# A graph kernel's second aggregation: six PSUM banks for the sums, two shared by the pairs' products, and weighted one-hots in batches of eight

## The chip, the cores and the metric

The kernel runs on one core of a Trainium2 chip. The metric is the device time of one execution in microseconds (us).

## The reference

Four blocks act in turn on x (6250 nodes, 256 columns, float32): a graph layer, a feed-forward layer with eight experts, a second, weighted graph layer with a small MLP behind it, and a second expert layer. 100,000 edges connect the nodes. The change lies in the third block:

```python
def _L1_gnn_ref(h6_all, edge_index, edge_weight, W, b, W1, b1, W2, b2):
    N = h6_all.shape[0]
    row, col = (edge_index[0], edge_index[1])
    sl = jnp.arange(N, dtype=edge_index.dtype)
    row_sl = jnp.concatenate([row, sl])
    col_sl = jnp.concatenate([col, sl])
    ew_sl = jnp.concatenate([edge_weight, jnp.ones((N,), dtype=edge_weight.dtype)])
    deg = jax.ops.segment_sum(ew_sl, row_sl, num_segments=N)
    dinv = jnp.where(deg > 0, jax.lax.rsqrt(deg), 0.0)
    norm = dinv[row_sl] * ew_sl * dinv[col_sl]
    xw = h6_all @ W
    msgs = xw[col_sl] * norm[:, None]
    h7 = jax.ops.segment_sum(msgs, row_sl, num_segments=N) + b
    h = jax.nn.relu(h7 @ W1 + b1)
    out = h @ W2 + b2
    return out
...
x = x + _L0_gnn_ref(_layernorm(x, axis=-1), src, dst, L0_gnn_W_src, L0_gnn_gamma, L0_gnn_beta)
x = x + _L0_ffn_ref(_layernorm(x, axis=-1)[None], L0_ffn_W1, L0_ffn_b1, L0_ffn_Wg, L0_ffn_bg, L0_ffn_Wd, L0_ffn_bd)[0]
x = x + _L1_gnn_ref(_layernorm(x, axis=-1), edge_index, edge_weight, L1_gnn_W, L1_gnn_b, L1_gnn_W1, L1_gnn_b1, L1_gnn_W2, L1_gnn_b2)
x = x + _L1_ffn_ref(_layernorm(x, axis=-1)[None], L1_ffn_Wg, L1_ffn_bg, L1_ffn_bias, L1_ffn_W1, L1_ffn_b1, L1_ffn_W2, L1_ffn_b2)[0]
```

## The kernel before, in words

Nodes are held in 49 tiles of 128. The edges, sorted by the node that receives the sum, are cut into 830 items (ITEMS) of at most 128 edges of one tile. An aggregation treats one item at a time:

- POOL gathers 128 rows of 256 floats from DRAM with an indirect DMA into one of 12 ring buffers (`aggregate_gpsimd`, L772). Gather i waits until the sum of item i-12 is made.
- DVE makes a one-hot matrix, 128 edges x 128 nodes of the tile.
- PE multiplies it with the gathered rows into a PSUM bank (`aggregate_tensor`, L761; in the trace each float32 matmul is two records).
- DVE adds the bank into the tile's accumulator (`add_sums`, L728), whose offset it reads into registers once in eight items.

Each engine runs a program of its own, in order, and waits on semaphores. `sum_made` counts PE's sums, `added` DVE's adds. The first layer's aggregation (some 150 to 1467 us) takes four banks by turns and makes unweighted one-hots for eight items with one instruction (`one_hots`, L713), in two halves of `hot1`. Beside it run other works of the set-up for the second layer, among them the comparison L783 and the product L785 on DVE. The second layer's aggregation (some 2996 to 4209 us) takes two banks and makes the one-hot of item i+2, times the edge weight, with one instruction per item (`one_hot`, L720), in four buffers.

What follows the sums in the second layer is done in pairs of tiles beside it, in `heads` of `second_vector`, `second_scalar` and `second_tensor`. A pair has steps 0 to 10, and a table of due items says beside which item each is issued. On this input it is `when_on_time` (L1591): step n of pair gi is due at item 17 x (tiles up to and with the pair) + 11 + 3n, so that a pair's steps are three items apart and pairs 34 items. The steps are: 0 scale by the degree (DVE, L1648); 1 transpose (PE, L1755, bank 2); 2 copy out (DVE, L1641); 3 product and bias (PE L1704, ACT L1696, bank 3); 4 the same with Relu (PE L1704, ACT L1687, bank 4); 5 third product (PE, L1735, bank 5); 6 add to x and statistics (DVE, L1632, L543); 7 normalize (DVE, L568); 8 transpose (PE, L1160, bank 6; ACT L1677); 9 gate product (PE, L1716, bank 7); 10 gate's bias and the search for the two best experts (DVE, L1608 to L1616). The loop goes on behind item 829 until the last pair is done; the last pair (gi = 24) is a single tile.

```python
m.wait_ge(ring_in[i % RING], 16 * (ring_loads(l, i % RING) + i // RING + 1))
if i >= nbank:
    m.wait_ge(added, l * ITEMS + i - nbank + 1)
m.matmul(bank[i % nbank][:, 0:width], lhsT=hot,
         rhs=ring[:, i % RING, 0:width], start=True, stop=True).then_inc(sum_made, 1)
beside(i)
```

## Time and profile before

| | us |
|---|---|
| median of 3 runs | 4848.15 (4842.85 to 4851.48) |
| the profiled execution | 4810.92 |
| its span | 4809.2 |
| busy in the span: PE, DVE, ACT, POOL | 3136.0, 2361.0, 1010.2, 2867.8 |
| mean granted clock of TensorE | 0.76 |

The span runs from the first to the last instruction of the profiled execution. Busy times are unions of an engine's instructions; those that only wait, branch or issue a DMA from another queue are not in them. In a group of instructions the idle time is that of the engine just before each of them, followed by what ended it; "issue" is idle time for which the profile shows no releaser, "remote" one that it can't name. The granted clock is a share of full speed: 1.0 is 2.4 GHz, 0.5 is 1.2 GHz.

### The profile page before, as it was taken

The numbers are of one execution on the slowest core, as the hardware profiler recorded it, in microseconds if no ns is written. First come the engines' busy times: TensorE is split into PE (matmuls) and PEld (weight loads), VectorE is DVE, ScalarE is ACT, GpSimd is POOL, SyncE is SP. The second block draws the span as 40 slices with busy tenths as digits, with TensorE's granted clock in tenths as the row PEclk, the third lists the DMA queues.
The fourth block names the chain that finished last, engine by engine and source line by source line (L and its number), as shares of the span: only waits on it lengthen the run. The fifth ranks groups of instructions, "written<-read, shape, count | busy, mean of one in ns | idle before, by whom it ended". The sixth has DMA issues, their size and how long they took to land.

```text
span 4809.2 us, 46065 instructions
## 1 busy us (share of the span) xinstructions
PE 3136.0 (65%) x11900; PEld 2202.3 (46%) x11900; DVE 2361.0 (49%) x5924; ACT 1010.2 (21%) x2504; POOL 2867.8 (60%) x2727
## 2 busy tenths in 40 slices
PE   4666778776772111067786872666666666669997
PEld 3555656655541111034466662344444444456555
DVE  6578777787861000144434115455555555553332
ACT  3444544444410000022230012000000000012221
POOL 1566777788877777700003661666666666647776
PEclk8777776678765555578897886678777877789999
DMA  3332333322231000011122334333333333433332
GB/s 122 91 89 74 90 90 90 90 84 80 80 84 38 1 1 1 1 70 57 70 79 72 108 103 148 97 98 103 100 104 100 100 104 100 99 118 56 53 56 45
DMA packets 201342, 378.28 MB, mean 79 GB/s; under 512 B 58955, under 2 KB 125783, under 8 KB 200696
## 3 DMA queue, kind: packets, MB, share of 16 engines
q0 software_dynamic: 134080, 283.48, 22.3%
q1 hardware_dynamic: 57964, 82.57, 4.9%
q10 hardware_dynamic: 9036, 9.15, 0.6%
q8 instruction: 114, 1.87, 0.2%
q14 instruction: 148, 1.21, 0.1%
HBM read 301.05 MB, written 75.83 MB: 78 GB/s over the span
## 4 chain that ended last, share of the span: by engine, by line
PE 40%; issue 17%; DVE 16%; another core or an unknown queue 13%; POOL 8%; DMA 3%; ACT 2%; DVEq 1%; SPq 0%; POOLq 0%; ACTq 0%
PE bank L761 18%; PE bank L1324 5%; DVE acc_or_weights L728 4%; PE bank L1513 4%; POOL out_rows L1930 3%; PE bank L1160 3%; PE bank L948 2%; POOL ring_or_weights L772 2%; PE bank L1704 2%; PE bank L1341 2%; POOL normed L1907 2%; POOL normed L1911 1%; PE bank L965 1%; DMA ring_or_weights<-gather_table,item_other_node 1%
## 5 line engine op out<-in xcount | busy, mean ns | idle before, releaser
L772 POOL DMA_INDIRECT ring_or_weights<-gather_table,item_other_node x1660 | 1753.4, 1056 | 830.7 <-issue 458.8
L728 DVE TENSOR_TENSOR acc_or_weights<-bank,acc_or_weights 128x257 f32 (+1 forms) x1660 | 704.3, 424 | 857.7 <-PE bank L761 450.8
L761 PE MATMUL bank<-ring_or_weights,normed 128*128 128x257 f32 x1660 | 769.2, 556 | 243.4 <-issue 162.5
L761 PE MATMUL bank<-ring_or_weights 128*128 128x256 f32 x1660 | 656.1, 513 | 386.3 <-DVE acc_or_weights L728 200.2
L1136 POOL DMA_INDIRECT items_by_src<-edge_records_by_src,edge_positions x542 | 553.7, 1022 | 169.1 <-issue 165.5
L761 PEld LDWEIGHTS bank<-ring_or_weights 128*128 128x128 f32 x1660 | 339.9, 241 | 658.8 <-issue 633.7
L948 PEld LDWEIGHTS bank<-normed,acc_or_weights 128*128 128x128 f32 x1564 | 393.2, 259 | 220.8 <-ACT acc_or_weights L941 90.4
L761 PEld LDWEIGHTS bank<-ring_or_weights,normed 128*128 128x128 f32 x1660 | 351.4, 260 | 309.0 <-issue 287.5
L1160 PE MATMUL bank<-identity,normed 128*128 128x128 f32 x1764 | 276.3, 288 | 281.9 <-DVE normed L568 221.6
L939 ACT ACTIVATE acc_or_weights<-iota_row,ring_or_weights 128x128 f32<-128x128 f32 x782 | 315.2, 403 | 647.5 <-PE bank L948 488.4
L948 PE MATMUL bank<-normed,acc_or_weights 128*128 128x49 f32 x1564 | 330.1, 301 | 89.1 <-ACT acc_or_weights L941 56.5
L1464 POOL DMA_INDIRECT normed<-hidden_rows,item_weight x56 | 54.7, 977 | 556.1 <-DVE item_weight L1413 537.8
L1160 PEld LDWEIGHTS bank<-identity,normed 128*128 128x128 f32 x1764 | 211.0, 146 | 375.8 <-DVE normed L568 144.3
L1174 PE MATMUL bank<-normed,ones 128*128 128x256 f32 x96 | 56.5, 690 | 401.2 <-issue 401.2
L720 DVE TENSOR_SCALAR ring_or_weights<-iota_row,item_local_node,item_weight 128x128 f32<-128x128 f32 x830 | 289.4, 349 | 3.2 <-issue 3.2
L1513 PE MATMUL bank<-acc_or_weights,normed 128*128 x896 | 226.0, 408 | 48.2 <-issue 30.6
L941 ACT ACTIVATE acc_or_weights<-acc_or_weights 128x128 f32<-128x128 f32 x782 | 243.6, 311 | 24.9
L1200 DVE SCALAR_TENSOR_TENSOR acc_or_weights<-acc_or_weights,normed 128x256 f32<-128x256 f32 x49 | 23.7, 484 | 430.6 <-issue 419.6
L1324 PE MATMUL bank<-ring_or_weights,normed 128*128 128x512 f32 x392 | 233.8, 753 | 0.0
L1174 PEld LDWEIGHTS bank<-normed,ones 128*128 128x128 f32 x96 | 23.8, 304 | 432.9 <-issue 432.5
L1513 PEld LDWEIGHTS bank<-acc_or_weights,normed 128*128 128x128 f32 x896 | 179.4, 206 | 79.9 <-issue 54.4
L1930 POOL DMA_INDIRECT out_rows<-normed,item_weight x105 | 169.3, 1612 | 76.3 <-issue 52.5
(348 smaller groups left out, 4106.1 us busy)
## 6 DMA issues: line engine op xcount, KB each, us to landing
ring_or_weights<-gather_table,item_other_node POOLq DMA_INDIRECT x1660
hidden_rows<-normed SPq DMA_DIRECT2D x49, 512.0 KB
items_by_src<-edge_records_by_src,edge_positions POOLq DMA_INDIRECT x542
acc_or_weights<-in_L_ffn_Wd SPq DMA_DIRECT2D x8, 1024.0 KB
acc_or_weights<-in_L_ffn_W SPq DMA_DIRECT2D x16, 512.0 KB, 9.8
gather_table<-normed SPq DMA_DIRECT2D x7, 896.0 KB, 4.1
gather_table<-acc_or_weights SPq DMA_DIRECT2D x7, 896.0 KB, 4.0
gather_table<-normed SPq DMA_DIRECT2D x24, 256.0 KB
```

What stands on the lines that cost most here:

```text
L720: v.tensor_scalar(onehot[:, i % 4, :], iota[:, :], dloc[:, i:i + 1], wt[:, i:i + 1], ALU.is_equal, ALU.mult).then_inc(hot_made, 1)
L728: v.tensor_tensor(into, bank[i % nbank][:, 0:width], into, ALU.add).then_inc(added, 1)
L761: m.matmul(bank[i % nbank][:, 0:width], lhsT=hot, rhs=ring[:, i % RING, 0:width], start=True, stop=True).then_inc(sum_made, 1)
L772: g.indirect_dma_start(ring[:, i % RING, 0:D], None, table, IndirectOffsetOnAxis(ap=gidx[:, i:i + 1], axis=0)).then_inc(ring_in[i % RING], 16)
L939: s.activation(lo_tmp, iota[:, :], ACT.Abs, bias=neg_lo[:, i:i + 1]).then_inc(lo_abs, 1)
L941: s.activation(lo_hot[:, i % 2, :], lo_tmp, ACT.Relu, bias=1.0, scale=-1.0).then_inc(lo_done, 1)
L948: m.matmul(bank[7][:, 0:T], lhsT=lo_hot[:, j % 2, :], rhs=tile_hot[:, j // HOTS % 2, j % HOTS, :], start=j == 0, stop=j == EC - 1).then_in ...
L1136: g.indirect_dma_start(item_d, IndirectOffsetOnAxis(ap=idx1[:, c:c + 1], axis=0), rec1[:, c, :], None).then_inc(edge_scattered[k], 16)
L1160: last = m.transpose(to[:, k * P:(k + 1) * P], rows[:, k * P:(k + 1) * P], ident[:, :])
L1324: last = m.matmul(bank[2 + half][:, :], lhsT=xt[:, u % 2, k * P:(k + 1) * P], rhs=w1a[:, k, cols], start=k == 0, stop=k == KD - 1)
L1513: last = m.matmul(bank[4 + u % 2][:, 0:D], lhsT=ht[:, u % 2, c * P:(c + 1) * P], rhs=wd[:, ds(regs[u // 4][u % 4] + c * D, D)], start=c == ...
L1930: g.indirect_dma_start(out, IndirectOffsetOnAxis(ap=to_row[:, u:u + 1], axis=0), ys1[:, u % 4, :], None, bounds_check=N - 1, oob_is_err=Fa ...
```

## The change

In the second layer six banks serve the sums. The steps of the pairs share banks 6 (PING: steps 1, 4 and 8) and 7 (PONG: steps 3, 5 and 9), and their waits are those for the last reader of the same bank. One-hots are made for eight items at once: a comparison as in the first layer, then a product in place with the edge weights, in two halves of a new buffer `hot2`. The last pair's due items are counted as if it had two tiles, 17 items later than before. The table for late input changes too; it isn't used here.

```diff
...
     ring = view(R, 0, RING * AW).rearrange("p (n a) -> p n a", a=AW)
-    after_ring = 4 * RING * AW
-    onehot = view(R, after_ring, 4 * P).rearrange("p (n c) -> p n c", c=P)
     def space(off, n, dt=F32, parts=P):
...
     xt2 = space(12288, 2 * G2 * D).rearrange("p (n a) -> p n a", n=2)
+    hot2 = space(24576, 2 * HOTS * P).rearrange("p (n c) -> p n c", c=P)
     norm2 = space(16384, 3 * G2 * D).rearrange("p (n t d) -> p n t d", n=3, d=D)
...
 
-    def one_hots(b):
+    HOT_BATCHES = -(-ITEMS // HOTS)
+    def one_hots(l, b):
         n = min(HOTS, ITEMS - b * HOTS)
+        cols = slice(b * HOTS, b * HOTS + n)
         if b >= 2:
-            v.wait_ge(sum_made, (b - 1) * HOTS)
-        at = b % 2 * HOTS
-        v.tensor_tensor(hot1[:, at:at + n, :], iota[:, :].unsqueeze(1).broadcast_to([P, n, P]),
-                        dloc[:, b * HOTS:b * HOTS + n].unsqueeze(2).broadcast_to([P, n, P]),
-                        ALU.is_equal).then_inc(hots_in, 1)
-
-    def one_hot(i):
-        if i >= 4:
-            v.wait_ge(sum_made, ITEMS + i - 3)
-        v.tensor_scalar(onehot[:, i % 4, :], iota[:, :], dloc[:, i:i + 1], wt[:, i:i + 1],
-                        ALU.is_equal, ALU.mult).then_inc(hot_made, 1)
+            v.wait_ge(sum_made, l * ITEMS + (b - 1) * HOTS)
+        hot = (hot1, hot2)[l][:, b % 2 * HOTS:b % 2 * HOTS + n, :]
+        equal = v.tensor_tensor(hot, iota[:, :].unsqueeze(1).broadcast_to([P, n, P]),
+                                dloc[:, cols].unsqueeze(2).broadcast_to([P, n, P]), ALU.is_equal)
+        if l == 0:
+            equal.then_inc(hots_in, 1)
+        else:
+            equal.then_inc(hots_in, 1)
+            v.wait_ge(hots_in, HOT_BATCHES + 2 * b + 1)
+            v.tensor_tensor(hot, hot, wt[:, cols].unsqueeze(2).broadcast_to([P, n, P]), ALU.mult).then_inc(hots_in, 1)
 
...
     def aggregate_vector(l, width, nbank, beside):
-        if l:
-            one_hot(0)
-            one_hot(1)
-        else:
-            one_hots(0)
+        one_hots(l, 0)
         regs = {}
         for i in range(ITEMS):
-            if l and i + 2 < ITEMS:
-                one_hot(i + 2)
-            if not l and i % HOTS == 1 and (i // HOTS + 1) * HOTS < ITEMS:
-                one_hots(i // HOTS + 1)
+            if i % HOTS == 1 and (i // HOTS + 1) * HOTS < ITEMS:
+                one_hots(l, i // HOTS + 1)
             beside(i)
...
         for i in range(ITEMS):
-            if l:
-                m.wait_ge(hot_made, i + 1)
-                hot = onehot[:, i % 4, :]
-            else:
-                m.wait_ge(hots_in, i // HOTS + 1)
-                hot = hot1[:, i % (2 * HOTS), :]
+            m.wait_ge(hots_in, HOT_BATCHES + 2 * (i // HOTS) + 2 if l else i // HOTS + 1)
+            hot = (hot1, hot2)[l][:, i % (2 * HOTS), :]
             m.wait_ge(ring_in[i % RING], 16 * (ring_loads(l, i % RING) + i // RING + 1))
...
     def when_late(gi, n):
-        return ITEMS + gi + n
+        return ITEMS + 12 * gi + n
 
     def when_on_time(gi, n):
-        return PER_TILE * min(T, G2 * (gi + 1)) + MARGIN + 1 + STEP * n
+        return PER_TILE * G2 * (gi + 1) + MARGIN + 1 + STEP * n
 
...
 
+    SUM_BANKS, PING, PONG = 6, bank[6], bank[7]
     def second_vector(when):
...
                 v.wait_ge(g_mm, gi + 1)
-                v.tensor_tensor(logits1[:, a:a + n, :], bank[7][:, 0:n * 8].rearrange("p (t e) -> p t e", e=8),
+                v.tensor_tensor(logits1[:, a:a + n, :], PONG[:, 0:n * 8].rearrange("p (t e) -> p t e", e=8),
                                 bg1.unsqueeze(1).broadcast_to([P, n, 8]), ALU.add).then_inc(g_out, 1)
...
                 v.wait_ge(x_mm, gi + 1)
-                v.tensor_tensor(X[:, a:a + n, :], bank[5][:, 0:n * D].rearrange("p (t d) -> p t d", d=D),
+                v.tensor_tensor(X[:, a:a + n, :], PONG[:, 0:n * D].rearrange("p (t d) -> p t d", d=D),
                                 X[:, a:a + n, :], ALU.add).then_inc(x_out, 1)
...
                 v.tensor_copy(at_b[gi % 2][:, :, 0:n * P],
-                              bank[2][:, :].rearrange("p (k n) -> p k n", k=KD)[:, :, 0:n * P]).then_inc(a_in, 1)
+                              PING[:, :].rearrange("p (k n) -> p k n", k=KD)[:, :, 0:n * P]).then_inc(a_in, 1)
             for gi in due(when, 0, i):
...
 
-        aggregate_vector(1, D, 2, beside)
+        aggregate_vector(1, D, SUM_BANKS, beside)
         for i in range(ITEMS, head_ends(when)):
...
                     s.wait_ge(g_mm, gi - 1)
-                s.activation(xt2[:, gi % 2, 0:n * D], bank[6][:, 0:n * D], ACT.Copy).then_inc(g_in, 1)
+                s.activation(xt2[:, gi % 2, 0:n * D], PING[:, 0:n * D], ACT.Copy).then_inc(g_in, 1)
             for gi in due(when, 6, i):
...
                 for c in range(KD):
-                    last = s.activation(ct_b[gi % 2][:, c, 0:n * P], bank[4][:, c * G2 * P:c * G2 * P + n * P],
+                    last = s.activation(ct_b[gi % 2][:, c, 0:n * P], PING[:, c * G2 * P:c * G2 * P + n * P],
                                         ACT.Relu, bias=bcol[:, 2 + c:3 + c])
...
                 for c in range(KD):
-                    last = s.activation(bt_b[gi % 2][:, c, 0:n * P], bank[3][:, c * G2 * P:c * G2 * P + n * P],
+                    last = s.activation(bt_b[gi % 2][:, c, 0:n * P], PONG[:, c * G2 * P:c * G2 * P + n * P],
                                         ACT.Identity, bias=bcol[:, c:c + 1])
...
                 m.wait_ge(g_in, gi + 1)
-                if gi >= 1:
-                    m.wait_ge(g_out, gi)
+                m.wait_ge(x_out, gi + 1)
                 for j in range(n):
                     for k in range(KD):
-                        last = m.matmul(bank[7][:, j * 8:(j + 1) * 8],
+                        last = m.matmul(PONG[:, j * 8:(j + 1) * 8],
                                         lhsT=xt2[:, gi % 2, j * D + k * P:j * D + (k + 1) * P],
...
                 m.wait_ge(applied2, gi + 1)
-                if gi >= 1:
-                    m.wait_ge(g_in, gi)
                 for j in range(n):
-                    last = transpose_rows(norm2[:, gi % 3, j, :], bank[6][:, j * D:(j + 1) * D])
+                    last = transpose_rows(norm2[:, gi % 3, j, :], PING[:, j * D:(j + 1) * D])
                 last.then_inc(g_tr, 1)
...
                 m.wait_ge(c_in, gi + 1)
-                if gi >= 1:
-                    m.wait_ge(x_out, gi)
                 for j in range(n):
                     for k in range(KD):
-                        last = m.matmul(bank[5][:, j * D:(j + 1) * D], lhsT=ct_b[gi % 2][:, k, j * P:(j + 1) * P],
+                        last = m.matmul(PONG[:, j * D:(j + 1) * D], lhsT=ct_b[gi % 2][:, k, j * P:(j + 1) * P],
                                         rhs=gcn_w[2][:, k, :], start=k == 0, stop=k == KD - 1)
...
                 m.wait_ge(b_in, gi + 1)
-                if gi >= 1:
-                    m.wait_ge(c_in, gi)
-                product(bank[4], gcn_w[1], bt_b[gi % 2], pairs[gi][1]).then_inc(c_mm, 1)
+                product(PING, gcn_w[1], bt_b[gi % 2], pairs[gi][1]).then_inc(c_mm, 1)
             for gi in due(when, 3, i):
...
                 if gi >= 1:
-                    m.wait_ge(b_in, gi)
-                product(bank[3], gcn_w[0], at_b[gi % 2], pairs[gi][1]).then_inc(b_mm, 1)
+                    m.wait_ge(g_out, gi)
+                product(PONG, gcn_w[0], at_b[gi % 2], pairs[gi][1]).then_inc(b_mm, 1)
             for gi in due(when, 1, i):
...
                 if gi >= 1:
-                    m.wait_ge(a_in, gi)
+                    m.wait_ge(g_in, gi)
                 for k in range(KD):
                     for j in range(n):
-                        last = m.transpose(bank[2][:, (k * G2 + j) * P:(k * G2 + j + 1) * P],
+                        last = m.transpose(PING[:, (k * G2 + j) * P:(k * G2 + j + 1) * P],
                                            acc[:, a + j, k * P:(k + 1) * P], ident[:, :])
...
 
-        aggregate_tensor(1, D, 2, heads)
+        aggregate_tensor(1, D, SUM_BANKS, heads)
         for i in range(ITEMS, head_ends(when)):
```

Where the order of instructions moves, the rows of both programs say it. In the following blocks each row is one instruction with the tiles it writes and reads; ISA at the add's line and TENSOR_LOAD are register work. First DVE in the second layer beside three items, before:

```order
L720 TENSOR_SCALAR ring_or_weights<-iota_row,item_local_node,item_weight 128x128 [waits rows_summed]
L728 ISA [waits added,rows_summed]
L728 TENSOR_TENSOR acc_or_weights<-bank,acc_or_weights 128x256
L720 TENSOR_SCALAR ring_or_weights<-iota_row,item_local_node,item_weight 128x128 [waits rows_summed]
L1657 TENSOR_TENSOR x_rows<-x_rows,edge_records_by_src 128x256
L96 TENSOR_LOAD item_acc_offset [waits bias_added]
L728 ISA [waits added,rows_summed]
L728 TENSOR_TENSOR acc_or_weights<-bank,acc_or_weights 128x256
```

And DVE of the changed kernel at the start of a group of eight items (its add is L730):

```order
L96 TENSOR_LOAD item_acc_offset
L730 ISA [waits added,rows_summed]
L730 TENSOR_TENSOR acc_or_weights<-bank,acc_or_weights 128x256
L716 TENSOR_TENSOR normed<-iota_row,item_local_node 128x1024 [waits rows_summed]
L723 TENSOR_TENSOR normed<-normed,item_weight 128x1024 [waits hots_set]
L730 ISA [waits added,rows_summed]
L730 TENSOR_TENSOR acc_or_weights<-bank,acc_or_weights 128x256
L730 ISA [waits added,rows_summed]
L730 TENSOR_TENSOR acc_or_weights<-bank,acc_or_weights 128x256
```

The one-hot in front of every add is gone; once in eight items two instructions of 1024 elements a partition stand between two adds. Then PE behind the last item, before (L1755 transposes of step 1, L1704 steps 3 and 4, L1735 step 5, L1160 step 8, L1716 step 9):

```order
L1735 MATMUL bank<-edge_records_by_src,normed 128x256 [waits head_x_out,head_c_in]
L1735 MATMUL bank<-edge_records_by_src,normed 128x256 x3
L1755 MATMUL bank<-identity,acc_or_weights 128x128 [waits head_sums_in,head_scaled]
L1755 MATMUL bank<-identity,acc_or_weights 128x128
L1160 MATMUL bank<-identity,normed 128x128 [waits head_n_in,head_normed]
L1160 MATMUL bank<-identity,normed 128x128 x3
L1704 MATMUL bank<-normed,edge_records_by_src 128x128 [waits head_b_in,head_sums_in]
L1704 MATMUL bank<-normed,edge_records_by_src 128x128 x3
L1716 MATMUL bank<-edge_records_by_src,normed 128x8 [waits head_gate_out,head_n_in]
L1716 MATMUL bank<-edge_records_by_src,normed 128x8 x3
```

The same place of the changed kernel (L1724 step 5, L1152 step 8, L1709 step 9, L1742 step 1, L1698 step 3):

```order
L1724 MATMUL bank<-edge_records_by_src,normed 128x256 [waits head_c_in]
L1724 MATMUL bank<-edge_records_by_src,normed 128x256 x3
L1152 MATMUL bank<-identity,normed 128x128 [waits head_normed]
L1152 MATMUL bank<-identity,normed 128x128 x3
L1709 MATMUL bank<-edge_records_by_src,normed 128x8 [waits head_x_out,head_n_in]
L1709 MATMUL bank<-edge_records_by_src,normed 128x8 x3
L1742 MATMUL bank<-identity,acc_or_weights 128x128 [waits head_n_in,head_scaled]
L1742 MATMUL bank<-identity,acc_or_weights 128x128
L1698 MATMUL bank<-normed,edge_records_by_src 128x128 [waits head_gate_out,head_sums_in]
L1698 MATMUL bank<-normed,edge_records_by_src 128x128 x3
```

The last tile's steps stood between those of the pair before; now they stand behind them.

## Rows read from the trace of the kernel before

**Rows 1.** The page: the span, and from its costliest groups the gathers and the adds.
```profile
span 4809.2 us, 46065 instructions
...
## 5 line engine op out<-in xcount | busy, mean ns | idle before, releaser
L772 POOL DMA_INDIRECT ring_or_weights<-gather_table,item_other_node x1660 | 1753.4, 1056 | 830.7 <-issue 458.8
```

**Rows 2.** Busy time by stretch (us): three of the first layer's aggregation, one of the second's.
```profile
core 0: us, PE busy (x) PEld busy (x) DVE busy (x) ACT busy (x) POOL busy (x), PEclk, DMA share, GB/s
160.00:400.00 240.00, 162.63 (x617) 122.38 (x616) 167.30 (x410) 108.03 (x303) 158.90 (x161) 0.74 0.30 89
600.00:850.00 250.00, 197.94 (x680) 157.66 (x680) 184.31 (x319) 120.75 (x338) 198.47 (x170) 0.68 0.31 90
1100.00:1440.00 340.00, 244.36 (x907) 174.80 (x908) 260.74 (x453) 114.84 (x322) 274.50 (x216) 0.75 0.30 81
3010.00:4200.00 1190.00, 815.79 (x2538) 515.77 (x2537) 660.28 (x2105) 56.94 (x138) 775.53 (x819) 0.77 0.35 100
```

**Rows 3.** Groups of instructions by form, 3010:4200 us.
```profile
line engine op names shapes xcount | busy us, mean ns | idle before us <-releasers
L772 POOL DMA_INDIRECT ring_or_weights<-gather_table,item_other_node x819 | 776.4, 948 | 414.6 <-issue 172.2 <-PE bank L761 172.2 <-remote 70.1
L761 PE MATMUL bank<-ring_or_weights 128*128 128x256 f32 x1626 | 642.9, 513 | 374.2 <-DVE acc_or_weights L728 198.5 <-issue 170.7
...
L720 DVE TENSOR_SCALAR ring_or_weights<-iota_row,item_local_node,item_weight 128x128 f32<-128x128 f32 x813 | 283.7, 349 | 0.0
```

**Rows 4.** The waits, 3010:4200 us.
```profile
engine line waited for: us in total, times, longest us
...
DVE acc_or_weights L728 <- PE bank L761: 304.2, 276, 3.4
PE bank L761 <- DVE acc_or_weights L728: 198.5, 151, 5.1
...
DVE acc_or_weights L728 <- remote: 148.4, 55, 5.5
```

**Rows 5.** Timeline, second layer: start us, duration us, instruction [idle before <-releaser].
```profile
3021.54 1.19 PE L761 MATMUL bank<-ring_or_weights 128*128 128x256 f32 x2 [3.00 <-issue]
...
3025.87 0.42 DVE L728 TENSOR_TENSOR acc_or_weights<-bank,acc_or_weights 128x256 f32 x1 [4.22 <-remote]
...
3026.44 1.19 PE L761 MATMUL bank<-ring_or_weights 128*128 128x256 f32 x2 [3.71 <-DVE acc_or_weights L728]
...
3030.77 0.42 DVE L728 TENSOR_TENSOR acc_or_weights<-bank,acc_or_weights 128x256 f32 x1 [4.22 <-remote]
3030.91 0.94 POOL L772 DMA_INDIRECT ring_or_weights<-gather_table,item_other_node  x1 [3.44 <-remote]
```

**Rows 6.** Groups, POOL, first layer: 160:400, 600:850 and 1100:1440 us, in this order.
```profile
L772 POOL DMA_INDIRECT ring_or_weights<-gather_table,item_other_node x161 | 160.7, 998 | 81.4 <-issue 32.7 <-PE bank L761 28.1 <-remote 20.6
...
L772 POOL DMA_INDIRECT ring_or_weights<-gather_table,item_other_node x170 | 199.1, 1171 | 51.8 <-issue 44.5 <-PE bank L761 7.0 <-remote 0.3
...
L772 POOL DMA_INDIRECT ring_or_weights<-gather_table,item_other_node x202 | 251.6, 1245 | 61.5 <-issue 50.0 <-PE bank L761 11.6
```

**Rows 7.** Timeline, first layer: gathers issued while DVE ran L783 or L713.
```profile
651.12 0.56 DVE L783 TENSOR_TENSOR normed<-iota_row,edge_positions 128x392 f32<-128x392 f32 x1
...
651.31 1.18 POOL L772 DMA_INDIRECT ring_or_weights<-gather_table,item_other_node  x1 [0.30 <-PE bank L761]
...
651.71 0.57 DVE L785 TENSOR_TENSOR normed<-normed,edge_records_by_src 128x392 f32<-128x392 f32 x1
...
671.57 1.22 DVE L713 TENSOR_TENSOR normed<-iota_row,item_local_node 128x1024 f32<-128x1024 f32 x1
671.63 1.98 POOL L772 DMA_INDIRECT ring_or_weights<-gather_table,item_other_node  x1 [0.30 <-issue]
```

**Rows 8.** Line L713: duration ns min/median/max, first and last start us, forms.
```profile
L713 DVE TENSOR_TENSOR normed<-iota_row,item_local_node x104: 948/1216/1225, 150.3 to 1430.1; 128x1024 f32<-128x1024 f32 x103, 128x768 f32<-128x768 f32 x1
```

**Rows 9.** Timeline, the tail of the second layer.
```profile
4209.02 0.42 DVE L728 TENSOR_TENSOR acc_or_weights<-bank,acc_or_weights 128x256 f32 x1 [0.73 <-PE bank L761]
...
4221.13 0.41 DVE L1641 COPY normed<-bank 128x256 f32<-128x256 f32 x1
...
4224.93 0.17 DVE L1608 TENSOR_TENSOR normed<-bank,edge_records_by_src 128x16 f32<-128x16 f32 x1 [3.39 <-PE bank L1716]
...
4234.56 0.16 DVE L1616 FIND_INDEX8 normed<-normed 128x8 uint32<-128x8 f32 x1
```

2 lines of the change are left out of this document (1 added, 1 removed).

## The prediction

> **What bounds the kernel now.** I began with the page: the span is 4809.2 us and the gathers of L772 head its costliest groups [rows 1]. The change touches only the second aggregation, so next came the table by stage. In the stretch 3010:4200, which holds nearly all of that stage, POOL is busy 775.5 of 1190 us, PE 815.8 and DVE 660.3, so no engine is full [rows 2]. The groups of that stretch say what one item costs: 819 gathers of 948 ns, each with its idle time in front, 414.6 us in all [rows 3]. Hence 1190/819 = 1.453 us an item.
>
> How much of that idle time is a wait? In the stretch 600:850 of the first layer 170 gathers have 51.8 us before them, 0.305 each, and in 1100:1440 it is 61.5/202 = 0.304 [rows 6]: that is what POOL itself takes between two gathers. So POOL's own pace is 0.948 + 0.305 = 1.253 us, and the rest, 414.6 - 819 x 0.305 = 165 us (167 for all 830 items), is POOL standing still because the ring of 12 is full. It is full because PE and DVE hold each other: PE waits 198.5 us for L728's adds [rows 4], which free one of two banks, and DVE waits 304.2 us for PE and 148.4 us for something the profile calls remote [rows 4]. The timeline shows the latter: a sum starts at 3021.54 and takes 1.19 us by its record, yet the add that follows comes at 3025.87 after 4.22 us of idle time, the next sum at 3026.44 after 3.71 us, and at 3030.77 and 3030.91 DVE and POOL are released together [rows 5]. PE reports late there, and with two banks nothing else can start meanwhile.
>
> **The change, part by part.**
>
> 1. Six banks instead of two. The sum of item i now waits for the add of item i-6. What can leave is the 167 us. Bounds come from the first layer, which has four banks and the same ring: in 600:850 and 1100:1440 nothing is left over 0.305 us a gather; in 160:400 it is 81.4 - 161 x 0.305 = 32.3 us, 0.20 a gather, which over 830 would be 167 us, all of it [rows 6]. PE's busy share is 0.68 in the stretch that stalls, 0.79 and 0.72 in the two that don't [rows 2]. The second layer has 0.69 now, and with the same work in some 1160 us 0.70 to 0.71, beside the 0.72. I take a fifth as staying, 33 us, for two of three stretches show none: -134 us. The bounds are -167 and 0.
>
> 2. One-hots in batches. Removed are 830 L720 of 349 ns, 290 us of DVE. Added are 104 times two instructions over 1024 elements. The first has the form of L713, 1216 ns [rows 8]; no row shows the second (a product with the weights) at that size, but over 392 elements it takes 0.57 us against 0.56 for the comparison [rows 7], so 1216 again: 104 x 2.43 = 253 us. DVE gets 37 us less, which lies beside PE and POOL and counts nothing.
>
> 3. What the batches do to POOL is the real price. A gather issued 0.06 us after L713 began took 1.98 us, not 0.95, and ended 0.82 us after L713's end [rows 7]. A gather issued s after the start is thus longer by 1.09 - s. Caught at any moment of a cadence of 1.25 us, that is 1.09 x 1.09 / (2 x 1.25) = 0.475 us a batch on average; caught at the start, 1.09. I take the middle, 0.78, since both happen and DVE's place in the cadence follows PE and DVE, not chance. For the second instruction the pair L783, L785 counts: a gather issued inside the first ended 0.82 us after the first's end, though the second was running [rows 7]. So it slips in between, and the next, 0.30 us later, is held by the second for about 0.03. Together 0.81 x 104 = +84 us, bounds 0.475 x 104 = 49 and 1.12 x 104 = 116. L720 was free of this: gathers beside it last 948 ns [rows 3].
>
> The Trainium skill, SBUF — State Buffer, section "Who interferes with whom", says that a DVE instruction with two SBUF inputs and a GpSimd instruction that reads SBUF exclude each other for the whole instruction. It speaks against this change, and the trace agrees with 1.98 us. Read as one lock over both instructions, it would hold a gather for 2.3 - s, on average 1.68 us a batch, an estimate of +175 us instead of +84; the gather of 651.31 decides against that reading.
>
> 4. The block on DVE. For 2.4 us no add runs, and the adds are what frees banks. At 1.35 us an item that is two items, and six banks (or the three items between two steps of a pair) cover it; with two they would not. Nothing is queued there for ACT that is due within three items. A batch is made seven items before PE needs it. At the stage's start batch 0 takes 2.4 us instead of 0.35, beside the first gather and its landing: nothing.
>
> 5. Sharing banks 6 and 7. PE's steps of a pair now wait for a reader of the same bank one or two steps earlier, at least three items before, or for the pair before, four or more items back. In the order nothing is queued closer, so zero while DVE is less than three items behind. It also means that PE leads DVE by three or four items near the steps, not six.
>
> 6. The last pair comes 17 places later, after the pair before is finished. The rows of the tail: the last add at 4209.02, pair 23's logits at 4224.93, the end at 4234.56 + 0.16 [rows 9]. Pair 23's gate product would come up to 1 us earlier without L1704 between, so its search ends by about 4224.7. Then the last tile runs alone: scale 0.34, transposes 0.4, and from its copy at 4221.13 to 4234.72, 13.6 us, less about 1 for the gate product that lay between. That is 4224.7 + 13.9 = 4238.6: +4 us (2 to 6).
>
> **Sum**: -134 + 84 + 4 = -46 us. The profiled execution took 4810.9 us and would take 4765. The median shown is 4848.2, 37 us above it; I carry the difference over: 4802 us.
>
> **Rivals.** (a) Slower: the lateness is PE's own and goes on with six banks, while the lock comes on top. For it speaks 160:400, four banks and 0.20 us of stall a gather [rows 6]; against it the later stretches. Place: PE's reports and the full ring. It decides from 47% of the 167 us staying (167 - 84 - 4 = 79). At three quarters: +46, 4894 us. Chance 0.19.
>
> (b) Slower: PE's granted clock sinks. It is 0.77 here and 0.68 to 0.75 in the first layer [rows 2], the mean of the levels 1.2 and 2.4 GHz. If it stayed at 0.5, an item would take the 1.19 us of [rows 5] and the pairs' work (815.8 - 642.9) x 0.77/0.5 = 266 us: 830 x 1.19 + 266 = 1254 us, above 830 x 1.453 = 1206: +52, 4900 us. It decides where PE's own time passes POOL's 1.35 us an item. The Trainium skill, TensorE: Matmul & The Clock Gate, section "A second HAM failure mode: psum-queue depth-cycling", tells of a kernel whose turns through PSUM banks with short PE idles between kept the clock going up and down. The trace has that up and down with two banks already. Chance 0.05.
>
> (c) The stalls and the lock about cancel (40 to 52% stay): within 10 us of now. Chance 0.10.
>
> (d) All stalls go and the lock costs its lower bound: -167 + 49 + 4 = -114, 4734 us. Chance 0.12.
>
> The forecast has the remaining 0.54.
>
> **Numbers.** A measurement here can tell about 0.2%, 10 us, from no change. Faster: 0.54 + 0.12 = 0.66; same 0.10; slower 0.24. The forecast's own ends: the lock at 116 with a third of the stalls staying (-111 + 116 + 4 = +9) and the lock at 49 with a fifth (-81). The range reaches on into (d) and into (a) up to about two thirds staying: 4745 to 4885.
>
> **What the profile after would show.** L772 in the second layer: mean near 1.05 us (right if 1.01 to 1.09) and idle near 0.35 us each; a mean of 0.95 would refute step 3, idle above 0.45 step 1. Gathers issued just behind a batch comparison last 1.9 to 2.0 us. PE's wait for the adds falls from 198.5 us to under 40. The stage falls from 1.453 to about 1.39 us an item, and the tail from the last add to the last search grows from 25.7 to about 30 us. Wrong altogether: if DVE still stands idle 4 us at a time for PE's reports and POOL stands with it.

## The result and the profile after

The change makes the kernel slower by a quarter of a per cent: 4860.8 us against 4848.7 (medians of 17 runs each), a ratio of 1.0026 with a 95% interval of 1.0016 to 1.0035. Forecast were 46 us less; it is 12 us more. The profiled execution took 4868.6 us, 58 more than that of before, but half of this is not the change: the second aggregation begins at 3025.1 us instead of 2996.3, and all of that stems from instructions that the change leaves alone (the first aggregation takes 1317 us in the profile of before and 1350 in that of the change, and 1310 to 1350 in all profiles of such chips below). The profile of before, 4810.9 us, is also not one of the 17 runs, whose fastest took 4835.6. So the stage itself is what to compare.

**Stage** means here from the start of the first gather of the second aggregation to the end of its last add, **stall** POOL's idle time before its gathers, from the second on, less 0.305 us each, and **tail** from that last add to the end of the last search. Before: stage 1213.1 us, stall 165, tail 25.3. After: stage 1230.0, stall 137, tail 32.1.

The page of the changed kernel, span and gathers of both layers, beside [rows 1]:

```profile
span 4866.8 us, 45372 instructions
...
L764 POOL DMA_INDIRECT ring_or_weights<-gather_table,item_other_node x1660 | 1790.9, 1079 | 814.9 <-issue 472.8
...
L716 DVE TENSOR_TENSOR normed<-iota_row,item_local_node 128x1024 f32<-128x1024 f32 x208 | 252.6, 1214 | 4.3 <-issue 3.6
```

Busy time in the stretch 3039:4229, the same part of the stage as 3010:4200 in [rows 2], with the same columns (the clock is the third number from the end, 0.75):

```profile
3039.00:4229.00 1190.00, 769.83 (x2507) 551.56 (x2506) 680.41 (x1473) 56.23 (x136) 807.96 (x810) 0.75 0.35 99
```

The groups of that stretch, which answer to [rows 3]:

```profile
L764 POOL DMA_INDIRECT ring_or_weights<-gather_table,item_other_node x810 | 808.4, 998 | 382.3 <-issue 185.8 <-remote 103.5 <-PE bank L753 93.0
L753 PE MATMUL bank<-ring_or_weights,normed 128*128 128x256 f32 x1603 | 553.8, 489 | 210.5 <-DVE acc_or_weights L730 128.5 <-issue 64.9 <-DVE normed L723 15.7
...
L730 DVE TENSOR_TENSOR acc_or_weights<-bank,acc_or_weights 128x256 f32 x801 | 339.1, 423 | 502.4 <-remote 212.4 <-PE bank L753 156.4 <-issue 66.2
```

The gathers' mean went from 948 to 998 ns. POOL's idle time per gather went from 0.506 only to 382.3/810 = 0.472 us; 0.35 had been expected. The gather line thus costs 1.470 us an item instead of 1.453. The idle time that was gained is smaller than what the gathers lost. The waits of the stretch, beside [rows 4]:

```profile
DVE acc_or_weights L730 <- remote: 212.4, 67, 8.1
...
DVE acc_or_weights L730 <- PE bank L753: 156.4, 127, 4.5
PE bank L753 <- DVE acc_or_weights L730: 128.5, 78, 4.8
...
PE bank L1724 <- ACT normed L1681: 52.3, 7, 11.8
PE bank L1698 <- ACT normed L1690: 48.5, 8, 8.7
```

PE's wait for the adds fell from 198.5 us, but to 128.5 and not under 40. New are PE's waits at the pairs' steps: with those for DVE (25.0, 16.1 and 10.5) and the 10.0 for ACT at L1709 they are 162 us, where before had none, and 15.7 us for the batches (L723). And DVE still stands for PE, now up to 8.1 us in one piece. The timeline shows such a piece (start us, duration us, instruction, idle before):

```profile
3816.66 1.99 PE L1698 MATMUL bank<-normed,edge_records_by_src 128*128 128x256 f32 x8 [1.12 <-issue]
3817.30 0.42 DVE L730 TENSOR_TENSOR acc_or_weights<-bank,acc_or_weights 128x256 f32 x1 [1.87 <-remote]
...
3818.49 1.46 PE L753 MATMUL bank<-ring_or_weights,normed 128*128 128x256 f32 x6
...
3819.45 0.42 DVE L730 TENSOR_TENSOR acc_or_weights<-bank,acc_or_weights 128x256 f32 x1 [0.27 <-PE bank L753]
...
3827.16 0.84 ACT L1681 ACTIVATE normed<-bank,bias_columns 128x256 f32<-128x256 f32 x2 [10.55 <-remote]
3827.30 0.42 DVE L730 TENSOR_TENSOR acc_or_weights<-bank,acc_or_weights 128x256 f32 x1 [7.42 <-remote]
3827.43 0.95 POOL L764 DMA_INDIRECT ring_or_weights<-gather_table,item_other_node  x1 [2.74 <-remote]
3828.05 3.06 PEld L1724 LDWEIGHTS bank<-edge_records_by_src,normed 128*128 128x128 f32 x8 [8.49 <-ACT normed L1681]
...
3828.47 1.22 DVE L716 TENSOR_TENSOR normed<-iota_row,item_local_node 128x1024 f32<-128x1024 f32 x1
3828.69 1.82 POOL L764 DMA_INDIRECT ring_or_weights<-gather_table,item_other_node  x1 [0.31 <-issue]
3829.72 1.23 DVE L723 TENSOR_TENSOR normed<-normed,item_weight 128x1024 f32<-128x1024 f32 x1
3830.82 0.95 POOL L764 DMA_INDIRECT ring_or_weights<-gather_table,item_other_node  x1 [0.30 <-issue]
```

By its records PE had a pair's product (step 4) done at 3818.65 and three sums at 3819.95. ACT, DVE and POOL hear of them only at 3827.2 to 3827.4, all at once. In the trace the updates of `sum_made` for the three sums stand at 3827.18, 3827.22 and 3827.26, 0.04 us apart, though a sum is four PE instructions; in the second aggregation of before_again, on the second kind of chip below, no two of its updates are nearer than 0.43 us. So here sums seem to have been made before and told late. Free banks don't help: the sums that filled them are reported late too, and PE itself stands at step 5 for ACT, which stood for the product. The last four rows are the lock of step 3: a gather issued 0.22 us after L716's start ends 0.82 us after L716's end, while L723 is running. The one behind it is issued 1.10 us after L723's start, so late that the same rule (1.09 - s) costs it nothing: 0.95 us.

The tail:

```profile
4254.68 0.42 DVE L730 TENSOR_TENSOR acc_or_weights<-bank,acc_or_weights 128x256 f32 x1 [0.96 <-PE bank L753]
...
4287.04 0.16 DVE L1610 FIND_INDEX8 normed<-normed 128x8 uint32<-128x8 f32 x1
```

### The profile page after: what moved, and what is told of

The parts are those of the page before. It is cut to its first block, busy times and chain, and to the rows that moved or that the text cites. A ratio compares the mean times of both kernels' runs of the same rounds, so it can differ in the third digit from the quotient of the medians.

```text
span 4866.8 us, 45372 instructions
## 1 busy us (share of the span) xinstructions
PE 3090.0 (63%) x11900; PEld 2229.2 (46%) x11900; DVE 2391.3 (49%) x5302; ACT 1010.2 (21%) x2504; POOL 2895.4 (59%) x2727
## 4 chain that ended last, share of the span: by engine, by line
PE 31%; issue 25%; DVE 17%; another core or an unknown queue 14%; POOL 7%; ACT 2%; DMA 2%; DVEq 1%; SPq 0%; POOLq 0%; ACTq 0%
PE bank L753 10%; PE bank L1316 5%; PE bank L1505 4%; DVE acc_or_weights L730 4%; POOL out_rows L1917 3%; PE bank L1152 3%; PE bank L940 3%; PE bank L1698 2%; PE bank L1333 2%; POOL normed L1894 2%; POOL ring_or_weights L764 1%; POOL normed L1898 1%; PE bank L957 1%; DVE normed L716 1%
## 5 line engine op out<-in xcount | busy, mean ns | idle before, releaser
L764 POOL DMA_INDIRECT ring_or_weights<-gather_table,item_other_node x1660 | 1790.9, 1079 | 814.9 <-issue 472.8
L753 PE MATMUL bank<-ring_or_weights,normed 128*128 128x257 f32 (+1 forms) x3320 | 1339.7, 521 | 446.5 <-issue 201.0
L730 DVE TENSOR_TENSOR acc_or_weights<-bank,acc_or_weights 128x257 f32 (+1 forms) x1660 | 703.5, 424 | 873.9 <-PE bank L753 309.7
L753 PEld LDWEIGHTS bank<-ring_or_weights,normed 128*128 128x128 f32 x3320 | 731.7, 253 | 665.8 <-issue 527.2
L1128 POOL DMA_INDIRECT items_by_src<-edge_records_by_src,edge_positions x542 | 539.1, 995 | 183.5 <-issue 182.0
L940 PEld LDWEIGHTS bank<-normed,acc_or_weights 128*128 128x128 f32 x1564 | 383.3, 256 | 266.5 <-ACT acc_or_weights L933 147.6
L1152 PE MATMUL bank<-identity,normed 128*128 128x128 f32 x1764 | 278.4, 289 | 310.7 <-DVE normed L568 225.5
L1152 PEld LDWEIGHTS bank<-identity,normed 128*128 128x128 f32 x1764 | 208.5, 146 | 413.4 <-issue 162.9
L1505 PE MATMUL bank<-acc_or_weights,normed 128*128 x896 | 228.5, 411 | 44.8 <-issue 29.0
L716 DVE TENSOR_TENSOR normed<-iota_row,item_local_node 128x1024 f32<-128x1024 f32 x208 | 252.6, 1214 | 4.3 <-issue 3.6
L1879 PE MATMUL bank<-acc_or_weights,normed 128*128 x840 | 198.6, 379 | 1.7 <-ACT normed L1845 1.7
L1871 PE MATMUL bank<-acc_or_weights,normed 128*128 x420 | 199.3, 597 | 0.0
```

What stands on the lines that cost most here:

```text
L716: equal = v.tensor_tensor(hot, iota[:, :].unsqueeze(1).broadcast_to([P, n, P]), dloc[:, cols].unsqueeze(2).broadcast_to([P, n, P]), ALU.is ...
L730: v.tensor_tensor(into, bank[i % nbank][:, 0:width], into, ALU.add).then_inc(added, 1)
L753: m.matmul(bank[i % nbank][:, 0:width], lhsT=hot, rhs=ring[:, i % RING, 0:width], start=True, stop=True).then_inc(sum_made, 1)
L764: g.indirect_dma_start(ring[:, i % RING, 0:D], None, table, IndirectOffsetOnAxis(ap=gidx[:, i:i + 1], axis=0)).then_inc(ring_in[i % RING], 16)
L940: m.matmul(bank[7][:, 0:T], lhsT=lo_hot[:, j % 2, :], rhs=tile_hot[:, j // HOTS % 2, j % HOTS, :], start=j == 0, stop=j == EC - 1).then_in ...
L1128: g.indirect_dma_start(item_d, IndirectOffsetOnAxis(ap=idx1[:, c:c + 1], axis=0), rec1[:, c, :], None).then_inc(edge_scattered[k], 16)
```

## The experiments

The runs fell on several chips, and these are of two kinds. On the first kind the kernel before takes 4819 to 4849 us (medians; the result above is of this kind), on the second 4045 to 4051. The program and its data are the same. Each chip below served one group of runs only, so it is not shown whether the chip makes the difference or the state that it was in then. Every row names the kind, and its ratio is to runs of before on the same chip.

| run | kind | ratio to before (95% interval) | stage us | gather ns | stall us | tail us |
|---|---|---|---|---|---|---|
| before | 1 | | 1213.1 | 948 | 165 | 25.3 |
| the change | 1 | 1.0026 (1.0016 to 1.0035) | 1230.0 | 998 | 137 | 32.1 |
| banks2 | 1 | 1.0076 (1.0063 to 1.0089) | 1248.8 | 997 | 156 | 30.7 |
| banks3 | 1 | 1.0036 (1.0024 to 1.0048) | 1226.0 | 1006 | 128 | 30.2 |
| single6 | 1 | 1.0036 (1.0023 to 1.0048) | 1220.7 | 949 | 168 | 32.0 |
| half_sums_b | 1 | single run | 1210.7 | 1005 | 113 | |
| filler_b | 1 | single run | 1229.3 | 990 | 144 | 30.7 |
| after_again | 1 | 1.0037 (1.0020 to 1.0053) | 1218.7 | 992 | 130 | 34.1 |
| single6_b | 1 | 1.0031 (1.0007 to 1.0055) | 1218.3 | 950 | 163 | 32.0 |
| single2 | 1 | 1.0016 (1.0004 to 1.0028) | 1225.6 | 951 | 170 | 29.5 |
| step4 | 1 | 0.9999 (0.9985 to 1.0013) | 1214.3 | 951 | 163 | 36.1 |
| tail10 | 1 | 1.0025 (1.0010 to 1.0039) | 1225.0 | 999 | 132 | 33.0 |
| bn_warm | 1 | 1.0157 (1.0139 to 1.0175) | 1224.6 | 952 | 167 | 22.0 |
| before_again | 2 | single run | 1055.5 | 949 | 0 | 24.0 |
| filler | 2 | single run | 1094.8 | 996 | 0 | 30.3 |
| half_sums | 2 | single run | 1098.4 | 1001 | 0 | |
| short_products | 2 | single run | 1103.7 | 1008 | 0 | |
| ring24 | 2 | 0.9999 (0.9990 to 1.0008) | 1057.8 | 949 | 0 | 29.2 |
| six_ring22 | 2 | 1.0010 (1.0001 to 1.0018) | 1055.8 | 949 | 0 | 32.3 |
| batch_ring22 | 2 | 1.0140 (1.0124 to 1.0156) | 1106.1 | 1010 | 0 | 30.3 |

How far one kernel repeats on the first kind: the second aggregation of bn_warm is that of before, 1224.6 against 1213.1; after_again is the change, 1218.7 against 1230.0. Stage lengths closer than some 11 us are not told apart by one profile each; only the ratios, from many runs, can do better. Two profiles of one kernel differ by up to 7 us in the stall (137 and 130).

**Banks.** banks2 and banks3 are the change with

```diff
-    SUM_BANKS, PING, PONG = 6, bank[6], bank[7]
+    SUM_BANKS, PING, PONG = 3, bank[6], bank[7]
```

(2 in banks2).

> The change with two banks for the sums instead of six (banks 2 to 5 lie idle); batches, shared PING and PONG and the late last pair stay. Theory 1 (PE's late reports are its own, banks only let other work go on meanwhile, and the batches block DVE for 2.4 us): two banks are clearly worse than six, since PE can lead DVE by two sums only and stands still during each batch, 104 x about 1 us: the aggregation's stage takes 1260 to 1330 us against 1230 with six and 1213 before, the whole run 1.008 to 1.025 of before. Theory 2 (it is the six banks that hurt, by letting PE run ahead in bursts and reach a pair's next step before ACT and DVE have read the last one): stage 1213 to 1240 us, whole run 1.000 to 1.004.

> The change with three banks for the sums. Theory 1: between two and six, stage 1230 to 1270 us, whole run 1.002 to 1.012. Theory 2: as fast as six or faster, stage 1205 to 1230 us, whole run 0.996 to 1.002, and PE's waits for ACT and DVE at the pairs' steps (some 200 us in the change, none before) gone.

Three banks give the same as six: 1.0036 against 1.0026 and 1.0037. Two with the batches are slower, just below what theory 1 expected (1249 us of stage for its 1260, 1.0076 for its 1.008). It fits that DVE's 2.4 us now hold PE: its waits for the adds are 248 us instead of 128.5, and two banks without the batches (single2, below) have 1.0016. Theory 2 falls: its stage came (1226.0 us), but not its time as a whole; PE's waits for ACT at the pairs' steps are 72 us in banks3 instead of 111 to 122, not gone, and nothing is won by that.

**One-hots.** single6 has six banks, and this in place of the batch:

```diff
+    def one_hot(i):
+        if i >= 2 * HOTS:
+            v.wait_ge(sum_made, ITEMS + i - 2 * HOTS + 1)
+        v.tensor_scalar(hot2[:, i % (2 * HOTS), :], iota[:, :], dloc[:, i:i + 1], wt[:, i:i + 1],
+                        ALU.is_equal, ALU.mult).then_inc(hots_in, 1)
...
+            if l and i + 8 < ITEMS:
+                one_hot(i + 8)
```

> The change with its six banks, but with the one-hots of the kernel before, one instruction of 349 ns per item, made eight items ahead into the sixteen places of the new buffer. If the batches cost POOL the 0.050 us a gather that the profile shows (0.998 against 0.948), the gathers' mean falls back to 0.948 and the stage to 1230 - 41 = 1189 us, the whole run to 0.994 of before. If DVE's own time is what matters (it has 37 us more here), the stage stays above 1215 and the run within 0.2% of the change. If the gathers' time is given back as idle time of POOL in front of a full ring, the mean falls and POOL's idle time above 0.305 us a gather rises from 137 to 160 us or more.

The third outcome came. The group of the gathers in single6, 3039:4229:

```profile
L774 POOL DMA_INDIRECT ring_or_weights<-gather_table,item_other_node x816 | 774.2, 949 | 416.8 <-issue 186.8 <-remote 155.9 <-PE bank L763 74.1
```

The gathers are back at 949 ns and the idle time rose from 0.472 to 0.511 us each. Per item 1.460 us: of the 0.049 us that the lock took, 0.039 came back as waiting. So here the lock lay almost wholly beside time in which POOL would have stood anyway.

single6 says as much on the banks. It is six banks without the batches, and its stall is 168 us (163 in single6_b); two banks without the batches have 165 (before), 167 (bn_warm) and 170 (single2). Six banks by themselves took nothing off the stall. The 137 us of the change are less because its gathers are longer. Only with the batches does the number of banks show, between two (156) and three (128).

**PE's work, first try.** From here on a third theory: PE's real pace, slower than its records, is the bound and follows its work. half_sums leaves out half of the sums' columns, filler adds a product of 128 columns ahead of each sum (with five banks for the sums), short_products leaves out most of the pairs' products. Of the two that leave work out only the stage's length is read. The edits, in this order (short_products shows two of its lines):

```diff
-                     rhs=ring[:, i % RING, 0:width], start=True, stop=True).then_inc(sum_made, 1)
+                     rhs=ring[:, i % RING, 0:w], start=True, stop=True).then_inc(sum_made, 1)
```

with `w = width // 2` in the second layer, and

```diff
+            if l:
+                m.matmul(bank[5][:, 0:P], lhsT=hot, rhs=ring[:, i % RING, 0:P], start=True, stop=True)
             m.matmul(bank[i % nbank][:, 0:width], lhsT=hot,
```

```diff
+            if not full:
+                return m.matmul(bk[:, 0:32], lhsT=w_sb[:, 0, 0:P], rhs=frm[:, 0, 0:32], start=True, stop=True)
```

> The kernel before once more, for how far two profiles of one kernel lie apart. Theory 3 (formed after the first three runs: the pace of the second aggregation is set by PE's real time per item, of which its records show a part only) needs stage lengths that repeat: 1213 us within 5. The first aggregation, whose code the change doesn't touch, took 1317 us in the profile of before and 1331 to 1350 in four others; if that is scatter it lands in 1330 to 1350 here too.

> The change, but PE multiplies only the first 128 of the 256 columns of every item in the second layer; DVE still adds 256, half of them old (half of each sum is left out, so only the stage's length is read, not the later stages). Theory 3 (PE's real pace is the bound, and its lateness goes with its work): POOL's idle time above 0.305 us a gather falls from 137 to under 50 us, late adds (over 2 us idle) from 77 to under 20, the stage from 1230 to 1090 to 1130 us. Rival (PE reports late because it does too little: the granted clock sinks and the reports get later still): clock under 0.70, idle time above 0.305 at 137 or more, stage 1230 us or more.

> The change with five banks for the sums and, ahead of every sum, one more product of 128 columns into the sixth, which nobody reads. Theory 3: PE gets 0.2 us (clock 1.0) to 0.4 us (0.5) more for each item, the stage grows by 830 times that, to 1390 to 1560 us. Rival (too little work makes PE late): the granted clock rises from 0.75 to 0.9 or more, late adds become rare and the stage falls to 1100 to 1220 us.

> The change, but from the second pair on the three products of a pair (steps 3, 4 and 5) are one product of 32 columns each instead of four of 256 (most of each product is left out, so only the stage's length is read). Theory 3: the pairs' products are some 170 us of PE by its records, and where PE is the bound most of that comes off: stage 1080 to 1140 us. Rival (the lateness comes from the sums and the start of bursts, not from the products): the late adds stay above 60 and the stage above 1200 us.

All four landed on the second kind of chip and answered another question. The gathers of before there, 2400:3400:

```profile
L772 POOL DMA_INDIRECT ring_or_weights<-gather_table,item_other_node x798 | 757.0, 949 | 243.1 <-issue 131.3 <-PE bank L761 111.8
```

243.1/798 = 0.305: POOL never stands, two banks or not, and the stage is 830 x (0.949 + 0.305) = 1041 us and its ends. What step 1 set out to win does not exist on this kind, and what step 3 costs is paid in full: the variants with batches have 996 to 1010 ns a gather and stages 39 to 51 us longer.

**PE's work, on the first kind.**

> The change with half-width products for the sums once more (half of each sum is left out; only the stage's length is read), because the four runs before this one were on a chip on which the kernel before takes 4045 us instead of 4840 and POOL never stood still (idle time above 0.305 us a gather: none, in all four). If this run is on a chip like the first (before 4840): theory 3 (PE's real pace, slower than its records, is the bound there and follows its work) expects the idle time above 0.305 to fall from 137 to under 50 us and the stage from 1230 to 1090 to 1130; its rival (too little work makes PE late) 137 us or more and 1230 or more. If it is on a chip like the second: 1098 us again, within 5.

> The change with the added product of 128 columns per item once more. On the second chip it raised the granted clock from 0.84 to 0.98 and cost nothing (stage 1095). On a chip like the first: theory 3 expects 830 times 0.2 to 0.4 us more, 1390 to 1560 us; the rival expects the clock at 0.9 or more, few late adds and 1100 to 1220 us.

> The change itself once more. On a chip like the first: stage 1230 us, whole run 1.0026 of before. On a chip like the second, where POOL's own pace is the bound and nothing hides the longer gathers: stage 1055 + 830 x 0.050 = 1097 us, the tail 7 us longer, so 1.011 to 1.013 of before.

> The change with one one-hot instruction per item. On a chip like the first: the gathers' 41 us go and POOL's idle time takes them back, whole run 1.0036 of before again, within 0.0015. On a chip like the second: gathers of 0.949 us, stage 1056 to 1060 us, whole run 1.001 to 1.003 of before (the later last pair is left).

The gathers and the busy times 3010:4200, half_sums_b first:

```profile
L765 POOL DMA_INDIRECT ring_or_weights<-gather_table,item_other_node x819 | 822.4, 1004 | 363.0 <-issue 183.8 <-remote 101.2 <-PE bank L754 78.0
3010.00:4200.00 1190.00, 675.71 (x2555) 556.39 (x2554) 692.60 (x1511) 56.97 (x138) 821.53 (x819) 0.62 0.36 101
```

and filler_b:

```profile
L766 POOL DMA_INDIRECT ring_or_weights<-gather_table,item_other_node x809 | 801.0, 990 | 389.4 <-issue 178.8 <-PE bank L755 131.7 <-remote 79.0
3010.00:4200.00 1190.00, 867.59 (x4101) 703.09 (x4102) 679.60 (x1472) 56.24 (x136) 800.84 (x809) 0.85 0.35 99
```

Both theories fall. Half of the sums' columns make 8 to 19 us, with the granted clock at 0.62 (mostly 1.2 GHz); half as many more with twice the PE instructions for sums cost nothing (1229.3 us beside 1218.7 and 1230.0), with the clock at 0.85. Neither the columns nor the number of instructions nor the granted clock are what makes PE late in this stage. after_again repeats the change (1.0037), single6_b repeats single6 (1.0031).

**What is left of the change without banks and batches, and the pairs' distance.** single2 is single6 with two banks, step4 is single6 with `STEP = 4`, tail10 is the change with

```diff
-        return PER_TILE * G2 * (gi + 1) + MARGIN + 1 + STEP * n
+        return PER_TILE * G2 * (gi + 1) - (10 if gi == HEADS - 1 else 0) + MARGIN + 1 + STEP * n
```

> The change with two banks for the sums and one one-hot instruction per item: of the change only the two banks that the pairs' products share and the later last pair are left. Theory 4 (six banks let PE reach a pair's next step before ACT and DVE have done the last, and it stands there with the sums behind it; that and the tail are the cost of the change): as fast as before but for the tail's 6 us, stage within 5 us of the 1213 of before and 1.000 to 1.002 of before as a whole. Rival (sharing the banks PING and PONG is what costs, whatever the number of sum banks): 1.003 to 1.005 as the change, single6 and banks3 have it. On a chip like the second: 1.001.

> single6 (six banks, one one-hot instruction per item) with the pairs' steps four items apart instead of three. Theory 4: PE's waits for ACT and DVE at the pairs' steps (some 200 us in the profile of the change, none in that of before) shrink to under 80 us, the stage falls from 1220 to 1195 to 1210 us and the run to 0.997 to 1.001 of before. Rival (those waits only stand where PE would be late anyway): no change against single6, 1.003 to 1.004. On a chip like the second: as single6 there.

> The change with the last pair's steps 10 places earlier (24 instead of 34 behind the pair before), as near as PING and PONG allow. From the last add to the last search 28 to 29 us instead of 30 to 34, the whole run 0.001 less than the change: 1.0015 to 1.003 of before.

single2 comes out at 1.0016, about the tail's share: 4 to 7 us are 0.001 of the run. That speaks for theory 4, weakly: its interval overlaps that of single6, and its stage is 1225.6 us, not within 5 of 1213 (nor is that of bn_warm, 1224.6, where the stage has the code of before). step4 gives 0.9999, in theory 4's range and the best version of this kind, no better than before; but the reason named for it is not borne out. PE's waits for ACT and DVE at the pairs' steps are 105.3 + 36.7 + 30.3 + 2.1 = 174 us in 1190, less than the 239 and 203 of single6 and single6_b but far from under 80, and the stage is 1214.3 us, above the 1195 to 1210 expected. So why step4 is 0.003 faster than single6, on another chip, is open. tail10's tail is 33.0 us and not 28 to 29: the moved steps did not shorten it, and its 1.0025 is the change's own.

**The late reports by themselves.** The batch norm's loop between the layers does little: per tile of nodes two float32 products of 128x256, two DVE and two ACT instructions. bn_warm is the kernel before with

```diff
         for t in range(T + 1):
+            for _ in range(4):
+                m.matmul(bank[3][:, 0:P], lhsT=ident[:, :], rhs=ident[:, :], start=True, stop=True)
```

> The kernel before, but in the batch norm's loop (1467 to 2050 us) PE makes four more products of 128 columns per tile, into a bank that nobody reads. On a chip like the first each tile takes 11.2 us there, 10.3 of them waiting for PE, at a granted clock of 0.5; on the second chip 0.86 us. If little work is what makes PE late: the loop shrinks from 580 us to 60 to 200 us and the run to 0.90 to 0.93 of before. If each product is late by itself, whatever goes on: three times the products, 25 to 34 us a tile, the run 1.15 to 1.25 of before. If the delay is one of time and not of products: no change, 1.00. On a chip like the second: 49 x 0.4 to 0.8 us more, 1.005 to 1.01.

In before, on the first kind, one turn of the loop takes 11.2 us (timeline, DVE):

```profile
1601.77 0.48 DVE L1200 SCALAR_TENSOR_TENSOR acc_or_weights<-acc_or_weights,normed 128x256 f32<-128x256 f32 x1 [10.26 <-issue]
...
1612.97 0.51 DVE L1200 SCALAR_TENSOR_TENSOR acc_or_weights<-acc_or_weights,normed 128x256 f32<-128x256 f32 x1 [10.25 <-issue]
```

On the second kind (before_again) the same turn takes 0.86 us:

```profile
1439.62 0.49 DVE L1200 SCALAR_TENSOR_TENSOR acc_or_weights<-acc_or_weights,normed 128x256 f32<-128x256 f32 x1
...
1440.48 0.48 DVE L1200 SCALAR_TENSOR_TENSOR acc_or_weights<-acc_or_weights,normed 128x256 f32<-128x256 f32 x1
```

In bn_warm the four added products wait for nothing, so PE's queue is hardly ever empty, and its records would show when it really takes each instruction:

```profile
1601.95 0.29 PEld L1171 LDWEIGHTS bank<-acc_or_weights,ones 128*128 128x128 f32 x1 [1.81 <-issue]
1602.65 0.58 PE L1171 MATMUL bank<-acc_or_weights,ones 128*128 128x256 f32 x1 [0.82 <-issue]
...
1604.05 0.29 PEld L1176 LDWEIGHTS bank<-normed,ones 128*128 128x128 f32 x1 [1.81 <-issue]
...
1605.45 0.58 PE L1176 MATMUL bank<-normed,ones 128*128 128x256 f32 x1 [2.22 <-issue]
...
1606.85 0.29 PEld L1176 LDWEIGHTS bank<-normed,ones 128*128 128x128 f32 x1 [2.51 <-issue]
...
1609.65 0.29 PEld L1168 LDWEIGHTS bank<-identity 128*128 128x128 f32 x1 [2.51 <-issue]
...
1611.05 0.37 PE L1168 MATMUL bank<-identity 128*128 128x128 f32 x1 [2.21 <-issue]
```

One instruction each 1.40 us, now and then 0.70, a weight load as well as a matmul of 256 or of 128 columns. A float32 product is four of them, two are 8 x 1.40 = 11.2 us: the turn of before. Six are 33.6 us, and so long did the turns of bn_warm take, 14 in a row. That is the second of the three expectations in pace (25 to 34 us a tile). The run as a whole grew by 1.6% only, because the spell ended by itself at about 2052 us, when 26 turns were still to go; those took 0.9 to 4.3 us. The spell began at 1510 us, and in before at about 1480, both with POOL already issuing its scatters (L1136) one each 1.27 us; its last scatter of that row in bn_warm started at 2040.36. In the stretch 2060:2400 of before POOL issues none, and the following 501 us, from the loop's end to the routing, take 492 on the second kind. That the two go together is seen; that POOL's scatters bring PE's spells about is not shown, for on the second kind POOL issues the same row and PE is quick.

This pace of one instruction each 1.40 us is the loop's. No row of the second aggregation shows it, and filler_b, with twice the instructions for the sums and the same stage, and the three updates 0.04 us apart speak against it there. What the two have in common is that PE's work is told late.

One rival is untested: the recording. In the profile of before the trace holds 1296 of the 1660 updates of `sum_made` and 1068 of the 1660 of `added`, in before_again 1658 and all. The missing ones fall where POOL issues indirect DMAs: between 2060 and 2400 us of before, where it issues none, no update is missing, in 3010:4200 PE has 730 of 949 and DVE 1137 of 1970. So on the first kind updates are lost from the record and PE is late in the same stretches, and on the second kind neither happens (2 updates of PE are missing of 3832). Whether one brings the other about, or a third thing both, no run can tell, as the times here all come from recorded executions. (The idle times that the profile calls "remote" stand where a wait ended and the update that ended it can be one of the missing.)

**A deeper ring.** ring24 is the kernel before with 12 more places for gathered rows in the second layer, six_ring22 and batch_ring22 are step4 and the change with 10 more (the edit is shown in part; the waits go by the deeper ring too):

```diff
+    more_ring = space(24576, MORE * D).rearrange("p (n a) -> p n a", a=D)
+    def ring_slot(l, i, width):
+        k = i % (DEEP if l else RING)
+        return ring[:, k, 0:width] if k < RING else more_ring[:, k - RING, 0:width]
```

> The kernel before with a ring of 24 places instead of 12 in the second layer (12 more in free space, nothing else changed). Theory 5 (PE is late in spells longer than the 12 places bridge, and quick between them): POOL's idle time above 0.305 us a gather falls from 165 us to 60 to 120, the stage from 1213 to 1110 to 1170 us, the run to 0.980 to 0.991 of before. Rival (PE's pace over the whole stage, spells and all, is the bound, two banks or six): the ring fills as before and the idle time stays at 150 us or more, 0.997 to 1.001. On a chip like the second: no change.

> step4 (six banks, one one-hot instruction per item, the pairs' steps four items apart) with a ring of 22 places. Theory 5: the banks help where the ring is deep, since PE then catches up at 0.43 us a sum instead of a sum per add with the wait between: idle time above 0.305 from 163 to under 60 us, 0.975 to 0.988 of before. Rival: as step4, 0.998 to 1.002. On a chip like the second: 1.001 to 1.003.

> The change with a ring of 22 places. Where the ring takes POOL's standing still away, nothing hides the longer gathers any more: the mean stays at 0.998 and the run comes out 0.007 to 0.009 above six_ring22. If the idle time stays, it is as the change, 1.0025 to 1.004. On a chip like the second: as the change there, 1.011 to 1.013.

These fell on the second kind, where no ring fills, so theory 5 was not tried. They price the batches, though, where nothing hides them: batch_ring22 takes 1.0140 and six_ring22 1.0010, with medians of 4106.3 and 4055.7 us 51 us apart, and the gathers of L791 and L801 differ by 830 x (1.010 - 0.949) = 51 us. batch_ring22, 2400:3400 (its ring lies in two tiles, hence two groups; this is one):

```profile
L791 POOL DMA_INDIRECT ring_or_weights<-gather_table,item_other_node x415 | 418.3, 1008 | 126.4 <-issue 78.3 <-PE bank L779 48.1
```

## Why the prediction was wrong, by its steps

1. **Six banks, -134 us: the step that failed.** By themselves they took off nothing: the stall is 168 and 163 us with six banks and single one-hots, 165, 167 and 170 with two. In the change it is 137, but those 28 us are the lock's, which lies beside the idle time (step 3). What the rows of the timeline said was read half: "PE reports late there, and with two banks nothing else can start meanwhile". The first half is the cause, the second was taken for it: sums in further banks are reported late as well, as the rows 3818.49 to 3827.30 show. The fraction that was to stay, a fifth, came from two quiet stretches of the first layer; the stretch 160:400 of [rows 6], with four banks and 0.20 us a gather, was the true neighbour, and 0.165 a gather is what stayed in the change, 0.20 in single6.

2. **DVE, 37 us less, counting nothing.** Right: L716 takes 1214 ns, L723 1226, as assumed (1216), and none of it shows.

3. **The lock, +84 us.** The mechanism was right to the hundredth: gathers issued s behind the comparison's start, up to 1.09 us, end 0.82 us after its end, though the second instruction is running, and the next gather is held by the second for some 0.01 us. The size was off by two: 830 x 0.050 = 41 us in the profile of the change. Between a cadence caught by chance (0.475 us a batch plus 0.03, 53 us) and one caught at the start I took the middle; chance was nearer, as the 41 us and the 51 us on the second kind of chip show. The lower bound was passed by 8 us. And it was added to the path at full price, though the same text had POOL standing idle for a wait that a longer gather can lie beside: single6 shows that four fifths of it did, 0.039 of 0.049 us a gather. The prediction had no term for this. The rule of the Trainium skill, SBUF — State Buffer, section "Who interferes with whom", holds for the comparison, but read as one lock over both instructions (175 us) it is refuted: the gather of 3828.69 ends at 3830.51, while L723 runs to 3830.95, where that reading would have held it to 3831.77.

4. and 5. **The block on DVE and the shared banks, 0 us.** With two banks the block does cost, as said (banks2, 1.0076 against 1.0016 of single2). Waits at the pairs' steps were not zero, 162 us in 1190. In the piece of the timeline they stand where a product is late anyway; that they all do is not shown, but no run shows a price for them beyond 0.002 of the run (single6 against single2, intervals that overlap).

6. **The last pair, +4 us (2 to 6).** It measured 6.8, above the upper bound; tails with the late pair are 29.5 to 36.1 us in thirteen profiles, tails in the old order 22.0 to 29.2 in four.

The sum with measured terms is 0 for the banks, +41 for the lock, -28 of it hidden, +7 for the tail: +20 us, against +17 and +7 in stage and tail of the two profiles, and +12 in the medians. A second pair, after_again and bn_warm (whose second aggregation and tail are those of before), has -6 and +12. So single profiles give the sum to some 20 us only. What came is rival (a), "the lateness is PE's own and goes on with six banks", in the words of the prediction: it decided from 47% of the stall staying, and 83% stayed in the change and all of it in single6. It had 0.19. The point against this rival, that later stretches of the first layer are quiet, was weak: they differ from the stretch in question in more than the number of banks. Rival (b) fell: the clock went from 0.77 to 0.75, and the stage doesn't follow it at 0.62 or 0.85. Of the signs named, the gathers' mean (0.998, below 1.01) missed its range, and the idle time (0.472, above 0.45) and PE's wait for the adds (128.5) said that step 1 was wrong, the idle time by the prediction's own bound. That the result is so near to none is luck in part: the batches cost 41 us of POOL and most of that happened to lie beside the stall.

**Open:** what makes PE late, in the aggregation and in the batch norm's loop, whether it is one thing, whether the recording has a part in it, and why only chips of the first kind have it; whether a ring of 22 or 24 places bridges the late pieces there; whether the six banks by themselves cost something on the first kind (single6 1.0036, single6_b 1.0031, single2 1.0016, step4 0.9999) beyond the tail. None of the versions is faster than the kernel before; step4 equals it on the first kind, ring24 on the second.

## What to carry to other kernels

A wait that ends in a late report of the engine that is waited for is not a wait for a buffer: before pricing more buffers at the whole wait, look whether the late instruction itself would have come sooner, and take the price from the stretch that stalls, not from those that don't. And when one part of a change takes 28 us off an idle time, look whether another part has filled it; the run with one of the two parts alone tells (single6). Don't add a cost on an engine that stands idle for 14% of the stage as if it never stood: what lies beside that idle time is free, until the idle time goes (41 us hidden for the most part on one kind of chip, 51 us paid in full on the other).

## What the runs showed of the hardware

- Two kinds of chip ran one program in 4045 to 4051 us and in 4819 to 4849 us. Some 505 us of the difference (from the first aggregation's end to the loop's end 555 us against 51) lie in the batch norm's loop and some 157 in the second aggregation (1213 against 1056).
- In the batch norm's loop on the first kind (bn_warm) PE takes one instruction each 1.40 us, at times 0.70, weight load or matmul, 128 or 256 columns. The granted clock reads 0.50 all through it, just as it does from 2426 to 2448 us of before_again, where no gather waits for PE, so the clock's rows don't show the spell. In before the records of a turn of that loop end at 1603.37 and ACT is released only at 1612.03: the others' idle times are the sign, not PE's records.
- In the second aggregation on the first kind PE's reports can come in bunches: a product and three sums within 0.13 us (3827.13 to 3827.26 of the change), 7.8 us after the report before. The stall stays with six banks (163 and 168 us), with half of the columns (113, beside 130 and 137) and with twice the instructions (144).
- A DVE comparison of 128x1024 that reads two SBUF operands holds back a gather issued beside it: it ends 0.82 us after the comparison's end. With a product of the same size right behind, that gather still ends while the product runs, and the next, issued 1.09 us after the product's start, takes 0.95 to 0.96 us. The Trainium skill, SBUF — State Buffer, section "Who interferes with whom", has the first half of this; the second only the trace shows.
